# Four small moves in a fused attention and quantised FFN kernel on eight cores: transposes two slots later, input copies, first columns and last product reordered

## What is computed

```python
def attn(x, w_qkv, w_proj):
    qkv = (x @ w_qkv.T).reshape(B, N, 3, 16, 128)
    q, k, v = qkv[:, :, 0], qkv[:, :, 1], qkv[:, :, 2]
    att = softmax(einsum('bnid,bnjd->bnij', q, k) * 128 ** -0.5)
    out = einsum('bnij,bnjd->bnid', att, v)
    return out.transpose(0, 2, 1, 3).reshape(B, N, 2048) @ w_proj.T

def ffn(x, kernel, bias):
    bq = fake_quant(bias, 8, -1)
    xq = fake_quant(x, 8, -1)        # one scale for each row
    kq = fake_quant(kernel, 8, 0)    # one scale for each column
    y = relu(xq @ kq + bq)
    return fake_quant(y, 8, -1)

x = x + attn(layernorm(x), w_qkv, w_proj)
x = x + ffn(layernorm(x), kernel, bias)
```

## Time and profile before

| what | us |
|---|---|
| median of 3 runs | 694.22 (693.73 to 694.78) |
| the profiled execution | 693.81 |
| its span on the slowest core, 3 | 692.3 |
| spans of the 8 cores | 687.5 to 692.3 |
| TensorE busy | 633.1 (91%) |
| VectorE, ScalarE busy | 352.0 (51%), 250.8 (36%) |

### The profile page before, as it was taken

The page is one execution under the profiler, slowest core; times in us unless marked ns, Lnnn a source line. Parts: engine busy times, 40 slices in busy tenths (PEclk is TensorE's granted clock), DMA queues, the critical chain, the costliest instruction groups (busy, mean ns, idle before and its releaser), DMA issues.

```text
span 692.3 us, 10316 instructions; the slowest of 8 cores (687.5 to 692.3 us)
## 1 busy us (share of the span) xinstructions
PE 633.1 (91%) x3712; PEld 322.3 (47%) x3712; DVE 352.0 (51%) x552; ACT 250.8 (36%) x501; POOL 34.6 (5%) x68
## 2 busy tenths in 40 slices
PE   0499999999999999999999997977987999999993
PEld 0354454554545454444445554544544544444441
DVE  3744344544455340101014577567767665566757
ACT  3851124323333321010104656557665643211121
POOL 0101000000000011111001000000000000000000
PEclk9999999999999999999999999899998999999997
DMA  8997789899999999999617115011101183111213
GB/s 249 262 214 159 153 210 212 191 184 229 227 192 215 206 168 163 156 166 158 97 29 122 62 62 172 12 62 62 60 3 62 62 267 160 61 62 62 122 62 121
DMA packets 20835, 95.11 MB, mean 137 GB/s; under 512 B 2353, under 2 KB 2353, under 8 KB 16945
## 3 DMA queue, kind: packets, MB, share of 16 engines
q0 software_dynamic: 9216, 33.56, 32.9%
q1 hardware_dynamic: 11570, 60.90, 26.8%
HBM read 111.21 MB, written 16.79 MB: 185 GB/s over the span
## 4 chain that ended last, share of the span: by engine, by line
PE 79%; ACT 8%; DVE 7%; issue 4%; DMA 1%; DVEq 0%; ACTq 0%; SPq 0%
PE pF L697 48%; PE pF L818 15%; PE pF L784 8%; ACT Ebuf L339 3%; PE pH L715 2%; DVE cols L543 2%; ACT zb L359 1%; PE pH L799 1%; DVE cols L501 1%; ACT zb L369 1%; DMA xbuf<-x_att 1%; DVE qx L555 1%; PE pF L732 1%; PE pF L733 1%; ACT aTT L349 1%
## 5 line engine op out<-in xcount | busy, mean ns | idle before, releaser
L697 PE MATMUL pF<-aT,wqb 128*128 128x512 bf16 x1536 | 338.2, 380 | 4.4 <-ACT aT L311 4.4
L697 PEld LDWEIGHTS pF<-aT,wqb 128*128 128x128 bf16 x1536 | 149.2, 98 | 179.7 <-issue 6.8
L784 PE MATMUL pF<-wpq,qT 128*128 128x512 bf16 x512 | 124.1, 389 | 4.0 <-DVE xr L529 4.0
L818 PE MATMUL pF<-kq,xqT 128*128 128x512 bf16 x512 | 111.2, 379 | 0.7 <-DVE xr L529 0.7
L818 PEld LDWEIGHTS pF<-kq,xqT 128*128 128x128 bf16 x512 | 49.9, 98 | 60.3 <-issue 0.9
L784 PEld LDWEIGHTS pF<-wpq,qT 128*128 128x128 bf16 x512 | 48.6, 100 | 54.4 <-issue 9.3
L339 ACT ACTIVATE Ebuf<-pF,cols 128x128 bf16<-128x128 f32 x128 | 45.4, 371 | 54.2 <-DVE cols L506 54.2
L455 DVE CAST vT<-pF 128x512 bf16<-128x512 f32 x16 | 11.1, 692 | 80.8 <-PE pF L697 80.8
L455 DVE CAST kT<-pF 128x512 bf16<-128x512 f32 x16 | 11.1, 692 | 64.9 <-PE pF L697 64.9
L565 DVE SCALAR_TENSOR_TENSOR tt<-pF,cols,bqb 128x512 f32<-128x512 f32 x32 | 24.0, 751 | 37.9 <-PE pF L818 37.8
L266 POOL DMA_DIRECT2D wqb<-wqkv x48 | 26.0, 543 | 311.9 <-PE pF L697 293.9
(11 more groups left out here) (70 smaller groups left out, 581.1 us busy)
## 6 DMA issues: line engine op xcount, KB each, us to landing
wqb<-wqkv POOLq DMA_DIRECT2D x48, 512.0 KB, 9.4
wkf<-wkT SPq DMA_DIRECT2D x16, 1024.0 KB, 10.3
xbuf<-x_att SPq DMA_DIRECT2D x8, 1024.0 KB, 16.7
kq_spill<-kqt SPq DMA_DIRECT2D x16, 512.0 KB, 9.7
wpq<-wp POOLq DMA_DIRECT2D x16, 512.0 KB, 11.5
xr<-x_res SPq DMA_DIRECT2D x8, 1024.0 KB, 5.3
kq<-kq_spill SPq DMA_DIRECT2D x4, 2048.0 KB, 13.0
out<-xr SPq DMA_DIRECT2D x7, 1024.0 KB, 4.3
```

The costliest lines, as they stand in the source:

```text
L697: mm = tn.matmul(pF[QBANK[j]][:, :], wqb[e % NW][:, 128 * c:128 * (c + 1)], aT[:, 8192 * h + 512 * c: 8192 * h + 512 * (c + 1)], start=(c ...
L784: mm = tn.matmul(pF[f % 2][:, :], sT[:, 2048 * b + 128 * m: 2048 * b + 128 * (m + 1)], wpq[u][:, 512 * m:512 * (m + 1)], start=(m == 0), s ...
L818: mm = tn.matmul(pF[y % 4][:, :], xqT[:, 2048 * k + 128 * c: 2048 * k + 128 * (c + 1)], w[:, c, :, :], start=(c == 0), stop=(c == NC - 1))
```

## The change

Four things are moved.

1. `l_transpose` and `l_evac` of each tile come two slots later (`r` = 4 and 5 on TensorE; 5 and 6 on ScalarE).
2. `at_evac(3)` comes ahead of the fifth tile's statistics and norm on both engines.
3. `HEADE` goes from 4 to 5; weight column `e` below 6 waits for input tile `e`, where columns 0 and 1 waited for tiles 2 and 3 and the others for nothing more; the two constants are loaded behind the first input tile. `JIDX`, and with it the point from which columns 6 to 10 are loaded, follows `JOBS`.
4. The last FFN product is two of 256 columns in two banks, and VectorE copies and takes the maximum of each by itself.

```diff
-HEADE = 4
+HEADE = 5
...
-            inc(sync.dma_start(ident[:, :], d_ident[:, :]), "cL", 16)
-            inc(sync.dma_start(neg[:, :], d_neg[:, :]), "cL", 16)
             for t in range(NT):
                 inc(sync.dma_start(xbuf[t][:, :],
                                    d_xatt[128 * t:128 * (t + 1), :]),
                     f"xL{t}", 16)
+                if t == 0:
+                    inc(sync.dma_start(ident[:, :], d_ident[:, :]), "cL", 16)
+                    inc(sync.dma_start(neg[:, :], d_neg[:, :]), "cL", 16)
...
-                if e == 0:
-                    g.wait_ge(S_("xL2"), 16)
-                elif e == 1:
-                    g.wait_ge(S_("xL3"), 16)
+                if e < NW:
+                    g.wait_ge(S_(f"xL{e}"), 16)
...
-            for t in range(NT):
+            for t in range(4):
                 norm(t)
                 if t >= 1:
                     at_evac(t - 1)
+            at_evac(3)
+            for t in range(4, NT):
+                norm(t)
+                if t >= 5:
+                    at_evac(t - 1)
             at_evac(NT - 1)
...
-                if r >= 3 and (r - 3) % 4 == 0 and (r - 3) // 4 < NT:
-                    l_evac((r - 3) // 4, 0)
-                if r >= 4 and (r - 4) % 4 == 0 and (r - 4) // 4 < NT:
-                    l_evac((r - 4) // 4, 1)
+                if r >= 5 and (r - 5) % 4 == 0 and (r - 5) // 4 < NT:
+                    l_evac((r - 5) // 4, 0)
+                if r >= 6 and (r - 6) % 4 == 0 and (r - 6) // 4 < NT:
+                    l_evac((r - 6) // 4, 1)
...
-            for t in range(1, NT):
+            for t in range(1, 4):
+                stats(t)
+                at_evac(t - 1)
+            at_evac(3)
+            stats(4)
+            for t in range(5, NT):
                 stats(t)
                 at_evac(t - 1)
...
-                if Y0 <= f:
+                if Y0 <= f < NS - 1:
...
-            wt(v, h_ev)
-            h_y2 = inc(v.reduce_max(cc(C_YM[k % 2] + 3), tt[k % 2][:, 1536:2048],
-                                    AX.X), "vS")
+            for h2 in range(2):
+                v.wait_ge(S_("yMM"), 4 * NT + h2)
+                cs = slice(1536 + 256 * h2, 1792 + 256 * h2)
+                h_ev = inc(v.scalar_tensor_tensor(
+                    tt[k % 2][:, cs], pF[3 + h2][:, 0:256], cc(C_SX[k]),
+                    bqb[:, cs], ALU.mult, ALU.add), "yEv")
+                wt(v, h_ev)
+                h_y2 = inc(v.reduce_max(cc(C_YM[k % 2] + 3 + h2),
+                                        tt[k % 2][:, cs], AX.X), "vS")
...
+            def y_last():
+
+
+                k, u = NT - 1, 3
+                w = kq[u].rearrange("p (f c n) -> p c f n", f=4, c=NC, n=128)
+                for h in range(2):
+                    if h == 0:
+                        tn.wait_ge(S_("yEv"), 4 * NT - 4)
+                    else:
+                        tn.wait_ge(S_("sEx"), NG)
+                    for c in range(NC):
+                        mm = tn.matmul(pF[3 + h][:, 0:256],
+                                       xqT[:, 2048 * k + 128 * c:
+                                           2048 * k + 128 * (c + 1)],
+                                       w[:, c, 2 * h:2 * h + 2, :],
+                                       start=(c == 0), stop=(c == NC - 1))
+                    inc(mm, "yMM")
...
-                if j < HEADE:
+                if j < 4:
                     a_transpose(4 + j)
...
-                    r = sl - P0 - 7
+                    r = sl - P0 - 9
                     if half == 1 and r >= 0 and r % 4 == 0 and r // 4 < NT:
                         l_transpose(r // 4, 0)
```

More of the change, by code:

```diff
@@ L135, in build_program @@
     C_SX = [252 + t for t in range(8)]
-    C_YM = [260 + 4 * i for i in range(2)]
+    C_YM = [260, 262]
     C_SY = [268 + t for t in range(8)]
@@ L649, in _ @@
             k = NT - 1
-            wt(v, h_ev)
-            h_y2 = inc(v.reduce_max(cc(C_YM[k % 2] + 3), tt[k % 2][:, 1536:2048],
-                                    AX.X), "vS")
+            for h2 in range(2):
[7 more added lines that the diff above has]
+                                        tt[k % 2][:, cs], AX.X), "vS")
             wt(v, h_y2)
-            h = inc(v.reduce_max(cc(C_YM[k % 2]), cc(C_YM[k % 2] + 1, 3), AX.X),
+            h = inc(v.reduce_max(cc(C_YM[k % 2]), cc(C_YM[k % 2] + 1, 4), AX.X),
                     "vS")
@@ L850, in _ @@
                         p_part((sl - P0) // 4, (sl - P0) % 4, c0, c1)
-                    else:
+                    elif sl < NS - 1:
                         y_part((sl - Y0) // 4, (sl - Y0) % 4, c0, c1)
+                    elif half == 0:
+                        y_last()
                     if half == 0 and 1 <= sl <= NG:
```

## The result

The changed kernel takes 706.5 us in the median of 4 runs (706.26 to 706.74), the one before 694.05 in the median of 4 beside it. The ratio is 1.0178, with a 95% interval of 1.0160 to 1.0196: 11.1 to 13.6 us slower, 12.4 in the middle. The forecast was 702.0 with a range to 707.5, so the result lies near its upper end.

The account below looks back on a forecast made before the run. It took a chain from centring through maximum, exponentials and rounding to the transposes to bound the 23.78 us periods. Waits 3.5, clock 2.4, head 1.5 and tail 0.4 sum to 7.8: 702.0 us against 694.22, range 695.5 to 707.5.

Parts of the forecast that it names:

- The wait that takes the place of the one removed: TensorE, before group 1's transposes: waits for ScalarE's copy behind the rounding, 6.7 us first, then 5.2, last 2.75 and 0.4.
- The period at full clock, 24.3 to 24.4 us: Four slots of the attention stretch: each full period costs 0.6 us more than the old 23.78.
- What the clock adds, +2.4: TensorE's granted clock: four falls on the slowest core, one more than before, at about 2.4 us each.
- the 3.5 of the waits: Stretch from attention to the last stage's first product: moved transposes cost +3.5 us at full clock.
- The head, +1.5: Kernel start: early weight columns delay the last input tile from 41.2 to 47.2 us, costing more than five columns first save.
- The forecast's lag: Head transfers: the POOL queue gets its first share about 4.5 us after its first column's issue.
- The bound on the gain without the early columns, -2.8: Head: if the input weren't delayed at all, the earlier start and the missing wait together make -2.8 us.
- The tail, +0.4: Last product in halves: two copies and two maxima behind VectorE's residual add take 2.04 us, not 1.64.
- The starved head (+4.3): Rival: weights take half the transfer engines at once, last input tile lands at 50.0, total 704.8 us; chance 0.12.
- The clock that wouldn't fall: Rival: waits of 5 us don't lower TensorE's clock, total 692.4 us, or 688 without a late head; chance 0.10.
- That the edit does what its order suggests: Rival: group 0's copy is out before TensorE comes, periods fall to about 19.2 us, total about 669; chance 0.04.

Follow-up runs that it names:

- e4_copies_first: Changed kernel with ScalarE copying the transposed rows out ahead of the slot's exponentials, centring and rounding; 684.53 us, ratio 0.9858 to the kernel before.
- e5_filled_wait: Changed kernel with 20 thrown-away matmuls of 512 columns put into each of the four long TensorE waits; 697.13 us, ratio 1.0042 to the kernel before.
- the edit alone: Kernel before with only the transposes and their copies two slots later; 703.56 us, ratio 1.0127.
- e7_head_weights_late: Kernel before with the head's edits, but weight columns still waiting for the third and fourth input tile; 690.70 us, ratio 0.9936.

## Why the prediction was right, point by point

**The wait that takes the place of the one removed.** Right: 6.7 forecast for the first, 6.3 seen; 5.2 for the next three, 5.26, 4.97 and 5.00 seen; 2.75 and 0.4 for the last two, 2.47 and 0.44 seen; six waits for the copy in place of five for `qx`. `e4_copies_first` shows the cause by changing only the copy's place.

**The period at full clock, 24.3 to 24.4 us.** Right: 24.4 in `e5_filled_wait`, where the clock stays up.

**What the clock adds, +2.4.** Right in kind, too small: this is the term that was mis-sized. The forecast priced a fall from the spans of two cores, 2.4 us, and counted four on the slowest core where there had been three, all of one size. All cores have the four. But on the slowest core a fall now costs 2.7 us, where the mean over the cores is 2.3, and the three before weren't all whole: at their windows' granted clock one was half as large as the others, and against undisturbed stretches they lost 6.6 us together: 2.7 and 1.3 in the first two periods (transposes at 432.62, 459.15, 484.24; 23.78 undisturbed) and 2.5 in the last (7.83 us between the two groups at 531.79 and 539.62, elsewhere 5.31). Four of 2.7 are 10.8, so the clock adds 4.2, not 2.4. With the 3.5 of the waits that makes 7.7; the profiles show 8.0 in this stretch and 0.4 behind it, and the edit alone 8.8.

**The head, +1.5.** Right in kind, 1 us too small: +2.5 in the profiles, +2.0 alone. The last tile was to land at 47.2 and lands at 48.2, and from there the steps are as forecast. Where the 1.0 comes from is open: on the eight cores the last tile lands between 47.4 and 49.6, and a first column issued earlier (7.1 to 8.9) doesn't go with a later landing. The forecast's lag held: the POOL queue moves its first data in the 13th microsecond, about 4.8 us after its issue at 7.47. The Trainium skill (DMA: Bandwidth & Descriptors, "Queues, rings and completion order") states that an engine goes round between the queues it has work for, one packet at a time. The trace agrees from 15 to 20 us (115 packets against 113, 50.9% and 50.7% of the time), but not in those first 4.8 us, in which the POOL queue got none. The bound on the gain without the early columns, -2.8, was a little small: in `e7_head_weights_late` the maximum over the first centred tile starts 3.0 us earlier on core 3 and 3.5 in the mean of the eight cores. What the timing shows beyond that, -4.4 (2.8 to 6.0), is open.

**The tail, +0.4.** Right in the trace (2.02 against 1.64 us); alone it is too small for the timing to tell.

**The rivals.** The starved head (+4.3) is out by the landing at 48.2. The clock that wouldn't fall is out by the four windows and by `e5_filled_wait`. That the edit does what its order suggests is out for the change, but `e4_copies_first` shows that a gain was there: with the transposes as late and only the copies' place altered, the kernel is 9.9 us faster than the one before.

Not settled is where the 1.2 us between the sum of the parts and the whole lie; the intervals of the four ratios cover it. The profiles have a stretch of about that size, the 1.3 us of the last transfers on the slowest core, which no version isolates.

## What to carry to other kernels

When an operation is moved in a hand-written order, look at what it lands behind in the queue of each engine that serves it: moving the transposes took away a wait of 3 us and put their copy behind a 2 us rounding that itself waits for two other engines. A wait of TensorE costs itself and what its clock loses; on this kernel waits of 5 us cost up to 2.7 us more each, so read the granted clock beside every wait. In a head where the transfer engines are full, issuing weights sooner delays the input (the last tile by 7.0 us here), and the input's chain is the one that is waited for.

## What the runs showed of the hardware that was not expected

- Waits of 3.0 to 3.2 us lowered TensorE's clock in 15 of 40 cases (five waits on each of eight cores; one to three falls on a core, spans 4.8 us apart), waits of 5.0 to 6.3 us in all 32 (0.974 to 0.976 on every core). Matmuls with a thrown-away result in the wait kept the clock at its upper level in most of them and gave back 9.4 us.
- A transfer issued on the POOL queue while the SP queue keeps the engines full got its first share 4.5 us (before) and 4.8 us (after) after its issue, and then about half of the engines' time, packet for packet.
- 32 matmuls of 256 columns take as long as 16 of 512: the group covers 3.66 us in the changed kernel; 16 of 512 cover 3.61.
